# First experts' layer: the copy of the next block's weights moved from ScalarE to VectorE

## The chip, the cores and the metric

One core of one Trainium2 chip. The metric is the device time of one launch of the whole program, in microseconds (us). A core has TensorE (PE; its weight loads are listed apart as PEld), VectorE (DVE), ScalarE (ACT), GpSimd (POOL) and SyncE (SP), which here only issues DMAs. SBUF is the memory on the chip with 128 partitions, PSUM the memory into which TensorE writes.

## The reference

Four layers over a graph of 3125 nodes with 256 features, all in float32: graph attention with a feed-forward network, a mixture of experts, a graph network of two steps, and a second mixture of experts. The change concerns the second, after the router:

```python
for e in range(E):                      # 8 experts, each token goes to 2
    h = jax.nn.gelu(tokens @ w1[e] + b1[e], approximate=False)
    y = h @ w2[e] + b2[e]
    out = out + combine[:, e:e + 1] * y
```

Here `w1[e]` and `w2[e]` are 256 x 256 each.

## The kernel before

The whole program runs its stages one after another. The first experts' layer is `experts(k, 0)` (L1692). Before it the router has given each (token, expert) pair a slot, the slots of one expert lie together, and they are padded to blocks of 256 rows. At most NBLK blocks exist, 30 of them run here, in an order that the chip has computed into the table `ORDER`: a word of it holds the block's slot number and its expert, and `block_of` (L1683) loads the word into registers of an engine (the load itself has line L430).

One block j is worked like this, with every tile double (index b):

- SyncE loads the 256 rows (`load_rows`, L1764), stores the output of block j-2 (`store`, L1775) and loads the bias row for the output (`load_rest`, L1769), in this order within its `step`. Its waits make the load of the next rows stand behind the store of an earlier output in the queue.
- TensorE turns the rows (`turn`, L1940) into `p_turned`; VectorE copies them from PSUM into `turned` (`copy_turned`, L1857).
- TensorE multiplies with the first weights (L1955) into `p_hidden`, in two halves; ScalarE applies the Gelu to each half (L1923) into `hidden`.
- TensorE turns the rows of block j+1, then multiplies `hidden` with the second weights (L1964) into `p_y`; VectorE adds the bias row to it (L1867) in two halves.

So TensorE's order is: first layer of j, turn of j+1, second layer of j, first layer of j+1, and so on.

The weights of all eight experts are loaded once, before the blocks, into the tile `every` (8 x 1026 columns: 512 for the first weights, 512 for the second, 2 for the first bias). The block's own expert must lie at a fixed place for TensorE, so before block j+1 its 1026 columns are copied from `every` to `pack[1 - b]`. Before the change ScalarE does that copy (`copy_weights`, L1912) at the head of its `step` for block j: it waits for `y_done` to reach j, that is until block j-1, the last user of that pack, is through its second layer, copies, signals `copied`, and only then applies the two Gelus of block j. TensorE waits for `copied` before each first layer. ScalarE copies the weights of block 0 ahead of the loop.

GpSimd meanwhile scatters the normalised rows into slots (L1823, 50 indirect DMAs, many of which are before the blocks start), then adds the residual in one TENSOR_TENSOR over all rows (L1833: 128 partitions x 6400 columns), and then gathers the outputs back (L1843) as they become available. The last gathers and VectorE's weighted sums (L1874, L1880) end the stage. The attention and the second experts' layer (`experts(k, 1)`, which loads its weights by DMA into `pack`) are not touched.

`half`, `over_blocks` and `over_odd` write out blocks 0 to 2 and loop over the others in pairs, on each engine alike.

Of the kernel before, what the change touches and what calls it, by code (L numbers as in the profile page):

```python
# [43 lines left out]
NEXP, TOPK = 8, 2  # L44
# [117 lines left out]
def wait_if(eng, sem, value):  # L162

    if not isinstance(value, int) or value > 0:
        eng.wait_ge(sem, value)
# [24 lines left out]
def at(i, n=1):  # L190
    return bass.ds(i, n)
# [234 lines left out]
def table_values(nc, engine, table, lo, most):  # L426


    why = "the chip computed the table within these bounds"
    values = nc.values_load_multi_w_load_instructions(  # L430
        table[0:1, at(lo, len(most))], engines=[engine], min_val=0, max_val=max(most),
        skip_runtime_bounds_check_because=why)[1]
    return [nc.s_assert_within(v, 0, m, skip_runtime_bounds_check_because=why) for v, m in zip(values, most)]
# [1249 lines left out]
def block_of(nc, engine, k, j):  # L1683


    word, = table_values(nc, engine, k["ORDER"], j, [511])
    why = "the chip computed the table within these bounds"
    return (nc.s_assert_within(word & 63, 0, NB - 1, skip_runtime_bounds_check_because=why),
            nc.s_assert_within(word >> 6, 0, NEXP - 1, skip_runtime_bounds_check_because=why))


def experts(k, layer):  # L1692
# [7 lines left out]
    nc, a, C, X, ST = k["nc"], k["a"], k["C"], k["X"], k["ST"]  # L1700
# [5 lines left out]
    G, B2 = B1 + HC, B1 + HC + 2 * KD  # L1706
# [3 lines left out]
    with ExitStack() as s:  # L1710
        def sb(what, shape, dt=F32):
            return s.enter_context(nc.sbuf_tensor(tag + what, shape, dt))

        def sem(what):
            return s.enter_context(nc.semaphore(tag + what))

        pack = k["PACK"] = [sb(f"pack{b}", [P, SIZE]) for b in range(2)]
        pack_in = k["PACK_IN"] = [sem(f"pack_in{b}") for b in range(2)]
        normed = sb("normed", [P, NT, D]) if layer else k["R"][:, 0:NT, :]
        every = None if layer else sb("every", [P, NEXP, G])  # L1720
        every_in, copied = sem("every_in"), sem("copied")
# [14 lines left out]
        hidden_done, gelu_done, y_done = sem("hidden_done"), sem("gelu_done"), sem("y_done")  # L1736
# [6 lines left out]
        order = Order(k, s, tag, pY[1][0], pY[1][1])  # L1743
# [6 lines left out]
        def over_blocks(eng, step):  # L1750
            n = eng.value_load(k["EPAIRS"][0:1, 0:1], min_val=2, max_val=NBLK // 2)
            over_odd(eng, n, step)
            return n

        @block.sync
        def _(sp):
# [33 lines left out]
            if not layer:  # L1790
                for e in range(NEXP):
                    sp.dma_start(every[:, e, :], a[name][e, :, 0:G]).then_inc(every_in, 16)
            sp.wait_ge(order.ready, 1)
            _, e = block_of(nc, mybir.EngineType.SP, k, 0)
            if layer:
                sp.dma_start(pack[0][:, 0:G], a[name][at(e), :, 0:G].squeeze(0)).then_inc(pack_in[0], 16)
# [49 lines left out]
        @block.vector  # L1846
        def _(dve):
            def copy_turned(j, b):
                dve.wait_ge(turned, j + 1)
                wait_if(dve, hidden_done, HC * (j - 1))  # L1850
                if affine:
                    dve.wait_ge(rest_in[b], 16 * (half[0] + 1))
                    for c in range(KD):
                        ins = dve.tensor_scalar(tT[b][:, c, :], pT[:, c, :], rest[b][:, c:c + 1],  # L1854
                                                rest[b][:, KD + c:KD + c + 1], ALU.mult, ALU.add)
                else:
                    ins = dve.tensor_copy(tT[b][:], pT[:])  # L1857
                ins.then_inc(tT_ready, 1)

            def step(j, b, i, first, last):  # L1860
                half[0] = i + b
                copy_turned(j + 1, 1 - b)
                dve.wait_ge(y_done, j + 1)
                dve.wait_ge(rest_in[b], 16 * (i + 1))
                wait_if(dve, y_out[b], 16 * i if not first else 0)
                for r in range(BR):
                    ins = dve.tensor_tensor(y[b][:, r, :], pY[b][r][:, 0:D], rest[b][:, B2 - G:], ALU.add)  # L1867
                ins.then_inc(y_ready, 1)

            def add_first(n):  # L1870
                dve.wait_ge(back_in[n], 16 * TOPK * (layer + 1))
                if not layer:
                    dve.wait_ge(residual, 1)
                dve.scalar_tensor_tensor(out=sums[n % RING][:], in0=back[:, n, 0, :], scalar=k["W12"][:, n, 0:1],  # L1874
                                         in1=X[:, n, :] if layer else normed[:, n, :], op0=ALU.mult,
                                         op1=ALU.add).then_inc(first_done, 1)

            def add_second(n):
                dve.wait_ge(first_done, n + 1)
                dve.scalar_tensor_tensor(out=X[:, n, :], in0=back[:, n, 1, :], scalar=k["W12"][:, n, 1:2],  # L1880
                                         in1=sums[n % RING][:], op0=ALU.mult, op1=ALU.add).then_inc(x_ready, 1)

            def spread_of(n):
                dve.wait_ge(x_ready, n + 1)
                dve.bn_stats(ST[:, n, :], X[:, n, :])

            def normalised(n):
                dve.tensor_scalar(normed[:, n, :], X[:, n, :], rstd[:, n:n + 1], nmr[:, n:n + 1], ALU.mult,  # L1888
                                  ALU.add).then_inc(normed_ready, 1)

            for n in range(2 * GN):
                normalised(n)
            order.vector(dve)
            for n in range(2 * GN, NT):
                normalised(n)
            dve.tensor_scalar(k["CSLOT"][:], k["SLOT"][:], float(NSLOT), None, ALU.is_lt).then_inc(slots_ready, 1)
            dve.wait_ge(slots_ready, 1)
            dve.tensor_tensor(k["CSLOT"][:], k["CSLOT"][:], k["SLOT"][:], ALU.mult).then_inc(slots_ready, 1)
            half = [0]
            copy_turned(0, 0)  # L1900
            over_blocks(dve, step)
            parts = (add_first, add_second) if layer else (add_first, add_second, spread_of)
            for n in range(NT + len(parts) - 1):
                for late, part in reversed(list(enumerate(parts))):
                    if 0 <= n - late < NT:
                        part(n - late)

        @block.scalar
        def _(act):
            def copy_weights(j, b):  # L1910
                _, e = block_of(nc, mybir.EngineType.Activation, k, j)
                act.copy(pack[b][:, 0:G], every[:, at(e), :].squeeze(1)).then_inc(copied, 1)  # L1912

            def step(j, b, i, first, last):
                if layer:
                    if not first:
                        act.wait_ge(y_done, j - 1)
                else:
                    wait_if(act, y_done, j)
                    copy_weights(j + 1, 1 - b)  # L1920
                for h in range(HC):
                    act.wait_ge(hidden_done, HC * j + h + 1)
                    act.activation(hid[b][:, h, :], pH[h % NH][:, 0:BT], ACT.Gelu,  # L1923
                                   bias=pack[b][:, B1 + h:B1 + h + 1]).then_inc(gelu_done, 1)

            act.activation(warm[:], k["EPSC"][:], ACT.Gelu)
            if not layer:
                act.wait_ge(order.ready, 1)
                act.wait_ge(every_in, 16 * NEXP)
                copy_weights(0, 0)  # L1930
            over_blocks(act, step)

        @block.tensor
# [488 lines left out]
```

## Time and profile before

| | |
|---|---|
| median of 3 runs | 2809.07 us (2808.21 to 2824.49) |
| the profiled execution, by the same clock as the runs | 2811.28 us |
| its span, from the first to the last instruction | 2809.5 us |
| granted TensorE clock over the span | 0.923 of full |
| busy: PE, DVE, ACT, POOL | 2291.3, 1475.0, 1228.3, 720.7 us |
| ScalarE's weight copies | 30, 1047 to 1052 ns each, 1399.9 to 1549.2 us |
| Blocks of the layer, first first-layer matmul to last bias add | 1413.4 to 1553.9 us |

All times of instructions are of that one execution and count from the start of its span. "Idle before", in brackets at the end of a timeline row, is the time that the engine stood before the instruction, with an arrow to what released it. A row with xN joins N instructions of one line. A granted clock of 1.00 is 2.4 GHz, 0.50 is 1.2 GHz.

### The profile page before, as it was taken

How to read it: one execution, taken by the hardware profiler on the slowest of the kernel's cores; microseconds unless marked ns; L12 is line 12 of the kernel's file. 1: busy time of each engine (PE TensorE's matmuls, PEld its weight loads, DVE VectorE, ACT ScalarE, POOL GpSimd, SP SyncE). 2: the span in 40 equal slices, each digit the busy share in tenths (PEclk: the TensorE clock that was granted, in tenths of full speed). 3: DMA queues.
4: the chain of work that ended last, by engine and by line, in shares of the span. 5: the costliest groups of instructions: out<-in, count | busy, mean ns of one | idle time of the engine just before them, and what ended most of it. 6: DMA issues, size and time to landing. Idle time of an engine off the chain costs nothing. (4 is left out here: it accounts for less than half of the span.)

```text
span 2809.5 us, 49979 instructions
## 1 busy us (share of the span) xinstructions
PE 2291.3 (82%) x10903; PEld 1803.6 (64%) x10904; DVE 1475.0 (53%) x2939; ACT 1228.3 (44%) x2503; POOL 720.7 (26%) x720
## 2 busy tenths in 40 slices
PE   2788876888888885997378399994999944999995
PEld 1344443666666663886367288883888843888885
DVE  7799975889898986334623644434001064111113
ACT  1799933777777771223233132223222241222221
POOL 0000012777777760002273311000110005102013
PEclk9899997999999998998589699996999956999998
DMA  5412222777777760000266322211222104656555
GB/s 199 195 74 76 76 83 89 208 213 212 213 212 213 212 183 36 1 0 4 85 200 185 107 67 69 71 55 54 71 67 73 49 2 173 218 192 220 191 206 178
DMA packets 183896, 353.27 MB, mean 126 GB/s; under 512 B 55347, under 2 KB 138728, under 8 KB 179112
## 3 DMA queue, kind: packets, MB, share of 16 engines
q1 hardware_dynamic: 138328, 206.94, 22.6%
q0 software_dynamic: 45520, 145.80, 18.2%
q8 instruction: 18, 0.29, 0.0%
q14 instruction: 30, 0.24, 0.0%
HBM read 275.32 MB, written 77.31 MB: 126 GB/s over the span
## 5 line engine op out<-in xcount | busy, mean ns | idle before, releaser
L2200 PE MATMUL gnn_p<-gnn_y,gnn_counts_wide 128*128 (+1 forms) x2500 | 553.0, 381 | 2.7 <-DVE R_kept L2135 2.5
L2200 PEld LDWEIGHTS gnn_p<-gnn_y,gnn_counts_wide 128*128 128x128 f32 x2500 | 472.5, 191 | 69.1 <-DVE R_kept L2135 6.8
L856 POOL DMA_INDIRECT kv_pair<-kv,gather_idx x448 | 427.9, 955 | 150.4 <-issue 101.2
L2071 ACT CAST gnn_counts_wide<-gnn_counts 128x1664 f32<-128x1664 uint16 x100 | 157.9, 1579 | 421.4 <-PE gnn_p L2200 403.7
L956 PE MATMUL p_edge_q<-QX_kept,onehot_turned 128*128 x904 | 264.2, 415 | 62.1 <-ACT onehot_turned L919 55.7
L1923 ACT ACTIVATE experts_hidden<-experts_p_hidden,experts_pack 128x256 f32<-128x256 f32 x290 | 134.3, 473 | 341.5 <-PE experts_p_hidden L1955 341.5
L1955 PE MATMUL experts_p_hidden<-experts_turned,experts_pack 128*128 128x256 f32 x1160 | 264.1, 383 | 2.1 <-DVE experts_turned L1854 1.2
L956 PEld LDWEIGHTS p_edge_q<-QX_kept,onehot_turned 128*128 128x128 f32 x904 | 155.2, 191 | 167.1 <-issue 151.6
L1964 PE MATMUL experts_p_y<-experts_pack,experts_hidden 128*128 128x256 f32 x1160 | 260.9, 380 | 0.0
L1955 PEld LDWEIGHTS experts_p_hidden<-experts_turned,experts_pack 128*128 128x128 f32 x1160 | 223.0, 192 | 33.7 <-issue 2.8
L564 PE MATMUL adj_p<-adj_onehot_src,adj_onehot_key 128*128 128x416 f16 x1200 | 234.4, 346 | 6.8 <-DVE adj_onehot_src L538 4.6
L964 PE MATMUL p_sums<-R_kept 128*128 128x264 f32 x896 | 236.7, 387 | 0.0
L1964 PEld LDWEIGHTS experts_p_y<-experts_pack,experts_hidden 128*128 128x128 f32 x1160 | 216.6, 191 | 27.2
L1843 POOL DMA_INDIRECT experts_back<-slots_out,CSLOT x100 | 97.6, 976 | 418.7 <-issue 417.3
L908 ACT ACTIVATE dst_distance<-WHERE_kept,DST_kept 128x128 f32 x456 | 158.3, 394 | 67.1 <-issue 67.0
L538 DVE TENSOR_SCALAR adj_onehot_src<-adj_count_src,adj_src_in_quarter 128x832 f16<-128x832 f16 x500 | 181.4, 430 | 0.0
L1854 DVE TENSOR_SCALAR experts_turned<-experts_p_turned,experts_rest 128x256 f32<-128x256 f32 x60 | 29.9, 540 | 276.5 <-DMA experts_rest<-experts 249.7
L564 PEld LDWEIGHTS adj_p<-adj_onehot_src,adj_onehot_key 128*128 128x128 f16 x1200 | 110.8, 99 | 96.2 <-issue 6.1
L883 DVE TENSOR_TENSOR qk_prod<-kv_pair,p_edge_q 128x528 f32<-128x528 f32 x224 | 156.5, 698 | 21.1 <-DMA kv_pair<-kv,gather_idx 13.9
L964 PEld LDWEIGHTS p_sums<-R_kept 128*128 128x128 f32 x896 | 153.2, 191 | 14.9 <-DVE ACC_kept L875 0.3
L2174 POOL TENSOR_TENSOR R_kept<-gnn_y,gnn_brows 128x256 f32 x50 | 39.3, 785 | 461.1 <-DVE gnn_y L2111 459.0
L888 DVE TENSOR_REDUCE qk_sum<-qk_prod 128x16 f32<-128x528 f32 x224 | 155.9, 696 | 0.0
(358 smaller groups left out, 3183.3 us busy)
## 6 DMA issues: line engine op xcount, KB each, us to landing
experts_pack<-experts SPq DMA_DIRECT2D x29, 2052.0 KB, 8.7
gnn_counts<-adj SPq DMA_DIRECT2D x400, 104.0 KB, 2.2
adj<-adj_counts SPq DMA_DIRECT2D x100, 208.0 KB, 1.9
experts_rows<-slots_in SPq DMA_DIRECT2D x60, 256.0 KB, 3.6
slots_out<-experts_y SPq DMA_DIRECT2D x58, 256.0 KB, 7.7
experts_rest<-experts SPq DMA_DIRECT2D x60, 130.0 KB, 7.4
kv_pair<-kv,gather_idx POOLq DMA_INDIRECT x448, 3.8
slots_in<-R_kept SPq DMA_DIRECT2D x2, 3328.0 KB, 14.0
```

The source lines that it names most:

```text
L538: ins = dve.tensor_scalar(ohs[p][:, c, :], count[:], column(smod, t + c), None, ALU.is_equal)
L564: mm = pe.matmul(pA[p][:, c, 0:QS // 2], ohk[p][:, n, :], ohs[p][:, n, c * (QS // 2):(c + 1) * (QS // 2)], start=False, stop=False)
L856: pool.indirect_dma_start(kv[r][:, j, :], None, a["kv"], bass.IndirectOffsetOnAxis(ap=idx[r][:, j:j + 1], axis=0)).then_inc(kv_in[r], 16)
L883: dve.tensor_tensor(prod[:], kv[r][:, :, 0:QW], pQ[q][:, :, 0:QW], ALU.mult).then_inc(prod_ready, 1)
L888: dve.tensor_reduce(red[q][:].rearrange("p j h -> p (j h)"), prod[:].rearrange("p j (h c) -> p (j h) c", c=HD + 1), AX.X, ALU.add).then_in ...
L908: ins = act.activation(dist[q][:, j, :], where[:, at(w), :].squeeze(1), ACT.Square, scale=-1.0, bias=column(k["DST"], t + j))
L956: mm = pe.matmul(pQ[q][:, j, 0:QW], oht[q][:, j, :], QX[:, at(w), :].squeeze(1), start=True, stop=True)
L964: mm = pe.matmul(pA[q][:, 0:VW], oh[r][:, j, :], wv[r % 4][:, j, :], start=(j == 0), stop=(j == GT - 1))
L1955: mm = pe.matmul(pH[c][:, 0:BT], w[:, lo:lo + P], tT[b][:, d, :], start=(d == 0), stop=(d == KD - 1))
L1964: mm = pe.matmul(pY[b][r][:, 0:D], hid[b][:, h, r * P:(r + 1) * P], w[:, W2 + h * D:W2 + (h + 1) * D], start=(h == 0), stop=(h == HC - 1))
L2071: act.copy(wide[b][:], raw[r][:].rearrange("p q s -> p (q s)")).then_inc(wide_ready, 1)
L2200: mm = pe.matmul(bank[:, off:off + D], wide[b][:, j * P:(j + 1) * P], y[:, at(n), :].squeeze(1), start=first and off == 0, stop=last and ( ...
```

## The change

VectorE gets `copy_weights`. In its `step` for block j it first copies the turned rows of block j+1, then the weights of block j+1, then adds the bias for block j. It waits for `y_done` to reach j before the copy, as ScalarE did. ScalarE's `step` holds only the two Gelus and waits for `copied` of its own block, because the bias in `pack` is an operand. The copy for block 0 goes to VectorE too, ahead of the first turned rows.

```diff
@@ VectorE @@
+            def copy_weights(j, b):
+                _, e = block_of(nc, mybir.EngineType.DVE, k, j)
+                wait_if(dve, y_done, j - 1)
+                dve.tensor_copy(pack[b][:, 0:G], every[:, at(e), :].squeeze(1)).then_inc(copied, 1)
+
             def step(j, b, i, first, last):
                 half[0] = i + b
                 copy_turned(j + 1, 1 - b)
+                if not layer:
+                    copy_weights(j + 1, 1 - b)
                 dve.wait_ge(y_done, j + 1)
                 dve.wait_ge(rest_in[b], 16 * (i + 1))
...
             half = [0]
+            if not layer:
+                dve.wait_ge(every_in, 16 * NEXP)
+                copy_weights(0, 0)
             copy_turned(0, 0)
             over_blocks(dve, step)
@@ ScalarE @@
-            def copy_weights(j, b):
-                _, e = block_of(nc, mybir.EngineType.Activation, k, j)
-                act.copy(pack[b][:, 0:G], every[:, at(e), :].squeeze(1)).then_inc(copied, 1)
-
             def step(j, b, i, first, last):
                 if layer:
                     if not first:
                         act.wait_ge(y_done, j - 1)
                 else:
-                    wait_if(act, y_done, j)
-                    copy_weights(j + 1, 1 - b)
+                    act.wait_ge(copied, j + 1)
...
             act.activation(warm[:], k["EPSC"][:], ACT.Gelu)
-            if not layer:
-                act.wait_ge(order.ready, 1)
-                act.wait_ge(every_in, 16 * NEXP)
-                copy_weights(0, 0)
             over_blocks(act, step)
```

## Rows read from the trace of the kernel before

**Rows 1.** The page, part 1: engine, busy us, share of the span, instructions.

```profile
PE 2291.3 (82%) x10903; PEld 1803.6 (64%) x10904; DVE 1475.0 (53%) x2939; ACT 1228.3 (44%) x2503; POOL 720.7 (26%) x720
```

**Rows 2.** Line L1857 alone, window 1451 to 1552: shortest, median and longest ns.

```profile
L1857 DVE COPY experts_turned<-experts_p_turned x22: 691/692/693, 1451.5 to 1551.3; 128x512 f32<-128x512 f32 x22
```

**Rows 3.** Timeline behind the loop, GpSimd's first gather there.

```profile
1557.43 0.95 POOL L1843 DMA_INDIRECT experts_back<-slots_out,CSLOT  x1 [27.72 <-issue]
```

**Rows 4.** Timeline of one block, 1455 to 1462: start us, length us, engine, line.

```profile
1455.33 0.66 PE L1940 MATMUL experts_p_turned<-C_kept,experts_rows 128*128 128x128 f32 x4 [0.54 <-DMA experts_rows<-slots_in]
...
1456.11 0.69 DVE L1857 COPY experts_turned<-experts_p_turned 128x512 f32<-128x512 f32 x1 [2.07 <-PE experts_p_turned L1940]
...
1457.33 1.70 PEld L1955 LDWEIGHTS experts_p_hidden<-experts_turned,experts_pack 128*128 128x128 f32 x8
1457.55 1.89 PE L1955 MATMUL experts_p_hidden<-experts_turned,experts_pack 128*128 128x256 f32 x8
1457.91 0.76 DVE L1867 TENSOR_TENSOR experts_y<-experts_p_y,experts_rest 128x256 f32<-128x256 f32 x2 [1.11 <-PE experts_p_y L1964]
1458.26 1.05 ACT L1912 COPY experts_pack<-experts_every 128x1026 f32 x1 [2.86 <-PE experts_p_y L1964]
1458.96 0.40 SPq L1775 DMA_DIRECT2D slots_out<-experts_y  x1
1459.21 0.83 ACT L1923 ACTIVATE experts_hidden<-experts_p_hidden,experts_pack 128x256 f32<-128x256 f32 x2
...
1459.91 0.66 PE L1940 MATMUL experts_p_turned<-C_kept,experts_rows 128*128 128x128 f32 x4 [0.47 <-DMA experts_rows<-slots_in]
1460.29 1.60 PEld L1964 LDWEIGHTS experts_p_y<-experts_pack,experts_hidden 128*128 128x128 f32 x8
...
1461.67 0.38 SPq L1764 DMA_DIRECT2D experts_rows<-slots_in  x1
```

**Rows 5.** The waits, window 1451 to 1553: us in total, times, longest.

```profile
PE experts_p_turned L1940 <- DMA experts_rows<-slots_in: 13.9, 21, 1.4
```

**Rows 6.** Groups by line of VectorE: busy us, mean ns; idle before.

```profile
L2111 DVE COPY gnn_y<-gnn_p 128x256 f32 x44 | 18.7, 425 | 191.2 <-PE gnn_p L2189 191.2
...
L2107 DVE COPY gnn_z<-R_kept 128x256 f32 x22 | 6.2, 283 | 0.0
```

**Rows 7.** Line L430 alone: VectorE's sequencer loading a table entry.

```profile
L430 DVEq TENSOR_LOAD <-GROUPS_kept x225: 299/305/346, 458.7 to 1049.3; - x113
```

**Rows 8.** Timeline, the stage's first turn and first layer.

```profile
1411.43 1.12 PE L1940 MATMUL experts_p_turned<-C_kept,experts_rows 128*128 128x128 f32 x4 [20.23 <-DMA experts_rows<-slots_in]
...
1413.42 3.75 PE L1955 MATMUL experts_p_hidden<-experts_turned,experts_pack 128*128 128x256 f32 x8 [0.88 <-DVE experts_turned L1857]
```

**Rows 9.** Timeline of GpSimd in the loop, around 1451.

```profile
1451.64 13.76 POOL L1833 TENSOR_TENSOR R_kept<-R_kept,X_kept 128x6400 f32<-128x6400 f32 x1 [1.81 <-DMA slots_in<-R_kept,SLOT]
```

**Rows 10.** Line L612 alone, window 368 to 382.

```profile
L612 DVE TENSOR_SCALAR h_row<-X_kept,RSTD_kept,NMR_kept x3: 395/5228/5324, 369.6 to 375.8; 128x256 f32<-128x256 f32 x3
```

**Rows 11.** The timeline there, both engines.

```profile
375.09 5.76 POOL L721 TENSOR_TENSOR WHERE_kept<-C_kept 128x3328 f32<-128x3328 f32 x1 [0.31 <-issue]
375.78 5.23 DVE L612 TENSOR_SCALAR h_row<-X_kept,RSTD_kept,NMR_kept 128x256 f32<-128x256 f32 x1 [0.53 <-PE p_hT L759]
```

**Rows 12.** Timeline of GpSimd, 1391 to 1400.

```profile
1394.26 4.91 POOL L1823 DMA_INDIRECT slots_in<-R_kept,SLOT  x1 [0.30 <-issue]
```

**Rows 13.** Line L1888 alone (VectorE): shortest, median and longest ns.

```profile
L1888 DVE TENSOR_SCALAR R_kept<-X_kept,RSTD_kept,NMR_kept x25: 393/396/412, 1381.8 to 1398.6; 128x256 f32<-128x256 f32 x25
```

**Rows 14.** Stretches: us, busy of PE, PEld, DVE, ACT, POOL, granted clock, DMA.

```profile
1553.00:1556.00 3.00, 0.00 (x0) 0.00 (x0) 2.81 (x8) 0.00 (x0) 0.00 (x0) 1.00 0.25 87
...
1557.00:1558.00 1.00, 0.00 (x0) 0.00 (x0) 1.00 (x4) 0.00 (x0) 0.56 (x1) 0.50 0.03 8
...
1419.00:1420.00 1.00, 1.00 (x5) 0.77 (x5) 0.00 (x0) 0.00 (x0) 0.69 (x2) 0.70 0.08 29
```

**Rows 15.** Groups by line in the stage, window 1411 to 1554.

```profile
L1823 POOL DMA_INDIRECT slots_in<-R_kept,SLOT x31 | 29.8, 962 | 9.4 <-issue 9.1 <-DMA slots_in<-R_kept,SLOT 0.3
```

## The prediction, made before the changed kernel was run

> **What bounds the kernel now.** The page first: 2809.5 us, one stage after another, with TensorE busy 82% of them [rows 1]. The change touches one stage, the 30 blocks of the first experts' layer. VectorE turns 22 of them over between 1451.47 and 1551.35 us, so one takes 99.9/21 = 4.76 us [rows 2], and with the 8 earlier ones the loop runs from 1413 to 1553 us: 140 us, 5% of the span. Nothing else runs beside it that could end the stage: the gathers behind the last blocks start only once the last output has landed [rows 3]. So a microsecond of the loop is a microsecond of the kernel.
>
> Then one block in the timeline [rows 4]. TensorE turns the next block's rows (1455.33), multiplies the second layer of this one (weight loads from 0.38 us after the turn, 1.60 us long), goes straight into the first layer of the next (1457.33, 1.70 us) and then stands until 1459.91, because the next rows have not landed. The waits say the same of the whole stretch: 13.9 us in 21 waits for `experts_rows` [rows 5], and none of TensorE for an activation in this stretch. Followed back, rows arrive late by a loop through the queue: output added (1457.91 to 1458.67), store issued (1458.96), then the rest of a pack and the table entries, next rows issued 2.71 us after the store (1461.67), landed, turned.
>
> ScalarE's copy of 1026 columns is 1.05 us and pushes the two activations back to 1459.21 to 1460.04. The second layer's first weights, which want the first activation (about 1459.7), load at 1460.29, behind the turn. The copy is therefore already hidden, with 0.6 us to spare for the first activation [rows 4].
>
> **The change part by part.**
> *ScalarE loses the copy and the wait for `y_done`.* 29 times 1.05 us of work go, and in the loop nobody waits for it; activations some 0.6 us earlier still find the second layer behind the turn. I take 0. A gain is bounded by the wait for rows: if all 13.9 us were in truth waits for activations, the whole of it scaled to 29 blocks would be 19 us; the row names the rows and I keep none of it.
>
> *VectorE gets the copy, 1026 columns, SBUF to SBUF.* This trace has the same operation with 256 columns in 283 ns, while from PSUM 256 columns are 425 ns and 512 are 692 ns [rows 2, 6]. From PSUM a column is 267/256 = 1.04 ns above a base of 158 ns. At half that per column the SBUF copy would be 158 + 133 = 291 ns, at the full rate 425: so it runs at twice the rate per column. 1026 columns are 158 + 535 = about 0.69 us; at the slow rate 1.23 us.
>
> *Where it lies.* It is queued behind the turned rows (0.69 us, starting 0.78 us after the turn). The table entry that it needs is loaded by the sequencer in 0.3 us [rows 7], beside the copy of the turned rows; not hidden it would be 0.3 us more. Instructions on VectorE overlap by some 0.07 us, so the copy ends 0.78 + 0.62 + 0.69 = 2.09 us after the turn's start. TensorE wants it at 2.00 us (1457.33 less 1455.33) [rows 4]: the first layer slips 0.1 to 0.2 us. TensorE stands 0.66 us a block for rows right after, so that is nearly all absorbed. Ends: 0 and 29 times 0.15 = 4.4 us; I take 0.5. The bias add behind it is due at 2.58 us after the turn, so it doesn't move, and neither does the store loop. The initial copy falls into the idle time before the first rows are turned (1411.43) [rows 8]: 0. Two waits are new. VectorE waits for `y_done` of the block before, which its own bias add has already waited for, so nothing queues behind it; ScalarE waits for `copied` of its own block, which TensorE needs before it can give ScalarE anything: 0 for both.
>
> *The new neighbour.* GpSimd runs one TENSOR_TENSOR over 6400 columns from 1451.64 to 1465.40, 13.76 us, in the middle of the loop [rows 9]. Elsewhere this trace shows what a VectorE instruction of the fast kind meets there. A TENSOR_SCALAR from SBUF to SBUF that takes 395 ns alone takes over 5.2 us twice; the one issued at 375.78 under a GpSimd TENSOR_TENSOR ends at 381.01, 0.16 us after GpSimd's instruction (380.85) [rows 10, 11]. The other way round, a GpSimd DMA_INDIRECT of 0.96 us took 4.91 us beneath VectorE's run of such TENSOR_SCALARs, while these stayed at 393 to 412 ns [rows 12, 13]. The two engines exclude each other for whole instructions. Today VectorE's two instructions in the loop read PSUM and don't care. No row shows a COPY stuck; the 283 ns put it among the fast kind.
>
> The Trainium skill, "SBUF — State Buffer", section Who interferes with whom, names it: copy, cast and tensor_scalar in a two-port mode take the port pair shared with GpSimd, and the one that issues second blocks until the first is done. The trace agrees for TENSOR_SCALAR (5.23 us instead of 0.40); that copies belong to it no row shows. By the rule the time is the forecast's, without it rival A's.
>
> *Its price.* The first weight copy that comes due u us after GpSimd's start ends 0.45 us after GpSimd: the stuck TENSOR_SCALAR ended 0.16 us after it, so 0.24 of its 0.40 us had been spent under the block, and I take as much off the 0.69 us. Unhindered it would end at u + 0.69. So it is 13.76 + 0.45 - 0.69 - u = 13.5 - u late. TensorE waits for it with the first layer, the bias add, store and next rows are queued behind it on VectorE. u is between 0 and one block, 4.76. In this trace the copy would come due at 1452.1, u = 0.45; but GpSimd's scatters before it are themselves held up by the new copies, by 0 to 8 times 0.69 = 5.4 us over eight blocks, which moves u freely. I take the middle, u = 2.4: 11.1 us, ends 8.7 and 13.5. Later copies of the loop are not under it.
>
> *TensorE's clock.* In the stall TensorE stands 9 to 13 us. Behind the loop TensorE has no work from 1553 on; the granted clock is 1.00 until 1556 and 0.50 in 1557 to 1558. At the stage's start, where it works from 1411.43, the clock is 0.70 in 1419 to 1420, on the rise [rows 8, 14]. So in the stall it falls to 1.2 GHz. At that level the first block's first layer took 3.75 us, and its turn 1.12 us, against 1.89 us and 0.66 us [rows 4, 8]. The block after the stall so costs 2 times 1.86 + 0.46 = 4.2 us more; the rows are there by then, which gives 0.66 back: 3.5 us. It could be none (the clock back at once) or the full 4.2 us.
>
> *GpSimd's other work* (scatters and gathers 0.69 us later at most, each time) is followed by no wait of the queue in the loop; 0.
>
> Sum: 11.1 + 3.5 + 0.5 = 15.1 us. On the profiled execution's 2811.3 us that is 2826.4; the median of the runs is 2.2 us below that execution, so 2824.2 us, 0.5% slower.
>
> **The rivals.**
> *A, no collision, not slower than before:* the copy finds GpSimd's long instruction no obstacle, the loop hides 0.69 us as it does now. For: no COPY stands stuck in a row of this trace. Against: the TENSOR_SCALARs of [rows 10, 11]. It decides at 1451.64 us: a weight copy under GpSimd of 0.7 us. Time 2809.07 + 0.5 = 2809.6.
> *B, slow rate, no collision:* the copy takes 1.23 us, ends 2.63 us after the turn, 0.65 to 0.75 us late for TensorE, whose 0.66 us of wait per block swallow most: 0 to 0.2 us a block over 29, some 3 us, 2812 us. Against: 283 ns [rows 6].
> *C, small collisions too:* the copies also wait for GpSimd's DMA_INDIRECTs, of which 31 scatters of 0.96 us alone lie in the stage [rows 15], and as many gathers follow. On perhaps 14 blocks half an instruction, 0.5 us, of which half is absorbed, and some of it also delays the bias add: 3 to 7 us more, about 2829 us. Against: 412 ns as the longest of 25 beside such instructions [rows 12, 13].
> *D, faster:* ScalarE, not the rows, holds the second layer back, and its 0.6 us a block come free: 17 us in 29 blocks, and no collision: 2792 us. For: nothing but the nearness of 1460.04 and 1460.29. Against: [rows 5].
>
> **How the numbers follow.** Forecast 0.78, A 0.07, B 0.05, C 0.08, D 0.02. The forecast's own range is 8.7 + 0 + 0 to 13.5 + 4.2 + 4.4 us, in practice 2818 to 2829. To hold 8 in 10 with the rivals it goes from 2814 (leaving A, B and D, 0.14, out) to 2831. One percent, 28 us, is about what a measurement of this kernel can tell from no change; only C with everything at its upper end, or a collision at a second place, passes it: 0.04. Faster by 1%: 0.01. Within: 0.95.
>
> **What would show it.** Right: one weight copy of VectorE between 9 and 14 us long that ends some 0.2 us after GpSimd's TENSOR_TENSOR, the others 0.69 us; TensorE idle over 8 us before a first layer in that stretch, and the granted clock at 0.50 for the block behind it; blocks elsewhere still 4.7 to 4.8 us apart and still ended by rows; a few scatters of GpSimd longer than 0.96 us. Wrong: all 30 copies near 0.69 us (A), near 1.23 us (B), copies of 1 to 2 us under scatters (C), or a loop pitch under 4.5 us (D). The clock term is wrong if first layers after the stall take 1.89 us.

## The result and the profile after

The changed kernel takes 2821.99 us (median of 7; 2820.45 to 2838.73) against 2808.83 us (median of 7; 2807.22 to 2824.49): ratio 1.006, 95% interval 1.0035 to 1.0085. That is 13 us slower; the forecast was 2824.2 us. A few executions of either kernel are some 16 us longer than the rest (one of the 7 before, two of the 7 after). The profiled execution took 2820.45 us with a span of 2818.7 us, 9.2 us more than the profiled execution before.

First the two copies in the loop, each line alone (count, shortest/median/longest ns, first and last start), profile after:

```profile
L1857 DVE COPY experts_turned<-experts_p_turned x30: 690/692/693, 1410.3 to 1558.8; 128x512 f32<-128x512 f32 x30
...
L1863 DVE COPY experts_pack<-experts_every x30: 689/698/10558, 1401.5 to 1559.5; 128x1026 f32 x30
```

29 of the 30 weight copies are near 0.70 us and one is 10.56 us. The loop, from the first turned rows to the end of the last bias add, is 151.0 us where it was 141.3 us. The timeline shows where the long copy lies:

```profile
1450.53 13.67 POOL L1833 TENSOR_TENSOR R_kept<-R_kept,X_kept 128x6400 f32<-128x6400 f32 x1 [2.10 <-DMA slots_in<-R_kept,SLOT]
...
1452.69 0.66 PE L1941 MATMUL experts_p_turned<-C_kept,experts_rows 128*128 128x128 f32 x4 [0.62 <-DMA experts_rows<-slots_in]
...
1453.48 0.69 DVE L1857 COPY experts_turned<-experts_p_turned 128x512 f32<-128x512 f32 x1 [2.50 <-PE experts_p_turned L1941]
...
1454.19 10.56 DVE L1863 COPY experts_pack<-experts_every 128x1026 f32 x1
1464.67 0.74 DVE L1874 TENSOR_TENSOR experts_y<-experts_p_y,experts_rest 128x256 f32<-128x256 f32 x2
...
1464.88 3.78 PE L1956 MATMUL experts_p_hidden<-experts_turned,experts_pack 128*128 128x256 f32 x8 [9.81 <-DVE experts_pack L1863]
...
1468.45 1.00 PE L1941 MATMUL experts_p_turned<-C_kept,experts_rows 128*128 128x128 f32 x4
...
1469.29 1.89 PE L1965 MATMUL experts_p_y<-experts_pack,experts_hidden 128*128 128x256 f32 x8
...
1470.23 0.74 DVE L1863 COPY experts_pack<-experts_every 128x1026 f32 x1
```

GpSimd's addition, the same as in [rows 9], ends at 1464.20. The copy, issued at 1454.19, ends at 1464.75, 0.55 us after it. The turned rows' copy at 1453.48 runs under the same GpSimd instruction and is not touched: it reads PSUM and takes its usual 0.69 us. Behind the long copy stand the bias add, the store and, through `copied`, TensorE, 9.81 us by its row. Then read how long TensorE's work takes: 3.78 us for the first layer and 1.00 us for the turn, but 1.89 us again for the second layer. The stretches say the same (granted clock third from the end):

```profile
1458.00:1459.00 1.00, 0.00 (x0) 0.00 (x0) 1.00 (x1) 0.00 (x0) 1.00 (x1) 1.00 0.00 0
1459.00:1464.00 5.00, 0.00 (x0) 0.00 (x0) 5.00 (x1) 0.00 (x0) 5.00 (x1) 0.50 0.00 0
...
1468.00:1469.00 1.00, 1.00 (x5) 0.78 (x4) 0.00 (x0) 0.30 (x1) 0.05 (x1) 0.50 0.14 44
1469.00:1471.00 2.00, 2.00 (x11) 1.62 (x9) 1.38 (x2) 0.17 (x1) 1.70 (x2) 0.93 0.61 152
```

The clock falls to 1.2 GHz in the stall. In 1469 to 1471 us it is 0.93 of full speed on average, so it came back at about 1469.3, 4.4 us after TensorE resumed. The waits from 1451 us on, against [rows 5]:

```profile
PEld experts_p_turned L1941 <- DMA experts_rows<-slots_in: 15.8, 19, 2.0
PE experts_p_hidden L1956 <- DVE experts_pack L1863: 9.8, 1, 9.8
PE experts_p_turned L1941 <- DMA experts_rows<-slots_in: 8.5, 13, 1.6
```

Rows still end the other blocks. The turned rows' copies span 148.5 us from the first start to the last, and the long block takes 16.1 us of them (1453.48 to 1469.59); the others are (148.5 - 16.1)/28 = 4.73 us apart, 4.79 before. ScalarE's freedom bought nothing that can be seen. Summed by stage, the 9.2 us between the two profiles are +9.7 in this loop, +1.6 in the first step of the GNN behind it (from the issue of its affine rows to the same issue in the second step), +1.5 in the untouched stages together, and -3.6 us between the start of the router and the first turned rows. That last stretch took 49.5 us in the profile before, 45.9 after, and 45.5 to 46.2 in six of the seven runs below that went to chips of the same speed. The profile before holds the scatter of 4.91 us of [rows 12] there, which stood under VectorE's TENSOR_SCALARs; the seventh run (e10, early rows with the whole addition) has one of 4.90 us and takes 49.9 us too. So the change did not earn these 3.6 us, and the 13.2 us between the medians are the better measure of it.

### The profile page after: what moved, and what is told of

Read it like the earlier page. It is cut to its first block and busy times, and to the rows that moved or that the text cites. A ratio compares the mean times of both kernels' runs of the same rounds, so it can differ in the third digit from the quotient of the medians.

```text
span 2818.7 us, 49981 instructions
## 1 busy us (share of the span) xinstructions
PE 2294.4 (81%) x10903; PEld 1800.4 (64%) x10904; DVE 1506.5 (53%) x2969; ACT 1202.6 (43%) x2473; POOL 718.0 (25%) x720
## 5 line engine op out<-in xcount | busy, mean ns | idle before, releaser
L1956 PE MATMUL experts_p_hidden<-experts_turned,experts_pack 128*128 128x256 f32 x1160 | 268.0, 387 | 13.2 <-DVE experts_pack L1863 10.8
```

The source lines that it names most:

```text
L1956: mm = pe.matmul(pH[c][:, 0:BT], w[:, lo:lo + P], tT[b][:, d, :], start=(d == 0), stop=(d == KD - 1))
```

## The experiments

My theory: VectorE's SBUF-to-SBUF copy and a GpSimd instruction exclude each other, and the stall with its clock is the loss. The rival: the place in VectorE's queue costs in every block. Times are compared with the kernel before on the same chip. The intervals below reach 4 to 7 us to either side, so differences of a few us are read from the stages of the profiles, of which each kernel has one.

**Leaving GpSimd's addition out.** In both kernels:

```diff
-                pool.tensor_tensor(normed[:], normed[:], X[:, 0:NT, :], ALU.add).then_inc(residual, 1)
+                pool.sem_inc(residual, 1)
```

> The changed kernel without GpSimd's residual addition (6400 columns; the output of the first experts' layer so lacks its residual), a mere signal in its place. Lock theory (VectorE's SBUF-to-SBUF copy and a GpSimd instruction exclude each other): the one copy of 10.56 us goes back to 0.70 us, all 30 lie between 0.69 and 0.90 us, the time falls from 2822 to 2808 to 2811 us. Rival (the place in VectorE's queue costs: the first layer slips about 0.5 us in every block, and the stall is only part of the loss): at least 3 us stay, 2812 to 2815 us.

> The kernel before, with the same piece of work left out. Both theories: no instruction of the loop waits for GpSimd there, so 2808 to 2810 us as before; it is the partner of the run above, and their difference is the price of moving the copy without any collision: under 1.5 us by the lock theory, 3 us or more by the rival.

Line L1863 alone in the changed kernel without the addition:

```profile
L1863 DVE COPY experts_pack<-experts_every x30: 686/698/922, 1400.9 to 1549.5; 128x1026 f32 x30
```

The long copy is gone, and the loop is 141.0 us with the moved copy and 140.7 us without it: 0.2 us for 29 blocks. The whole times, however, missed both expectations: 2819.84 us (ratio 1.0046, 1.0031 to 1.0062) and 2816.63 us (1.0031, 1.0015 to 1.0048) against 2807.44 us. In both runs the stretch from the second experts' layer's last turned rows to the end is about 46 us instead of 36, presumably because the missing residual changes what that layer routes. So the pair must be read against each other, and there 3.2 us stay, as the rival had it, though not in the loop. The profiles put them elsewhere, below.

**The copy at the single rate.** A form with one SBUF source that isn't of the fast kind:

```diff
-                dve.tensor_copy(pack[b][:, 0:G], every[:, at(e), :].squeeze(1)).then_inc(copied, 1)
+                dve.tensor_reduce(pack[b][:, 0:G], every[:, at(e), :].squeeze(1).unsqueeze(2), AX.X,
+                                  ALU.max).then_inc(copied, 1)
```

> The changed kernel with the copy written as a TENSOR_REDUCE (max over one element), a form that should run at the single rate: some 1.23 us instead of 0.70 for each of the 30, in the same place of the queue, with GpSimd's residual addition in place. Lock theory: the lock belongs to the fast kind alone, so none of the 30 is longer than 1.3 us, there is no stall, and the time is 2810 to 2817 us although VectorE works longer. Rival (whatever VectorE reads from SBUF under GpSimd's instruction is held up, or the queue is what costs): one copy over 9 us again, or 0.5 us more in every block, 2822 us or more.

The line alone, then GpSimd's and VectorE's timeline in that run:

```profile
L1863 DVE TENSOR_REDUCE experts_pack<-experts_every x30: 1222/1222/1224, 1399.6 to 1548.9; 128x1026 f32 x30
```

```profile
1447.65 13.74 POOL L1833 TENSOR_TENSOR R_kept<-R_kept,X_kept 128x6400 f32<-128x6400 f32 x1 [2.11 <-DMA slots_in<-R_kept,SLOT]
```

```profile
1452.62 1.22 DVE L1863 TENSOR_REDUCE experts_pack<-experts_every 128x1026 f32 x1
```

1.22 us under the full length of GpSimd's instruction, as everywhere else. VectorE works 0.52 us longer in every block and the kernel is faster: 2811.8 us, ratio 1.0025 (1.0005 to 1.0045), loop 142.4 us. Same place in the queue, same source and destination, same neighbour: what costs is the kind of the instruction, the fast COPY. The run changes rate and operation together, so it does not show which of the two matters. The rival falls for the loop.

**GpSimd's addition in 25 instructions.**

```diff
-                pool.tensor_tensor(normed[:], normed[:], X[:, 0:NT, :], ALU.add).then_inc(residual, 1)
+                for n in range(NT):
+                    ins = pool.tensor_tensor(normed[:, n, :], normed[:, n, :], X[:, n, :], ALU.add)
+                ins.then_inc(residual, 1)
```

> The changed kernel with GpSimd's residual addition in 25 instructions of 256 columns, one per tile of rows. Lock theory, the lock held for one instruction: a copy waits for the piece under way, 0.8 us at most, so the longest copy is under 2 us and the time 2808 to 2812 us. Rival (GpSimd keeps the pair over its back-to-back instructions, or it is the amount of its work that counts): a copy of about 10 us stays and with it 2822 us.

```profile
L1865 DVE COPY experts_pack<-experts_every x30: 686/698/1025, 1399.6 to 1547.8; 128x1026 f32 x30
```

The longest copy is 1.03 us, the loop 140.7 us, the time 2809.9 us, ratio 1.0019 (1.0002 to 1.0036). The lock (the exclusion of one engine by the other) is held for one instruction, and VectorE gets in between two of them; a piece of GpSimd that meets a copy takes up to 1.18 us instead of 0.72.

**The addition twice in a row** (the residual so counts double; the second waits for the first one's semaphore; one execution alone):

> The changed kernel with GpSimd's residual addition done twice in a row (the residual so counts double, the output of the layer is changed by that). Lock theory: the copy that comes due under the first addition waits for it, about 10 us as before; the second addition follows a semaphore later, so either the same copy also waits for it (one copy of 22 to 25 us) or the copy gets in between and the next one is stuck for 8 to 13 us (two long copies). Either way the stage is 9 to 14 us longer than the changed kernel's 151.0 us from first turned rows to last output. Rival (a single hiccup at the point where the scatters end, whatever GpSimd does next): 151 us again.

This run, the two with 19 and 22 idle instructions and the two with 48 memsets (e5, e6, e7, e11, e12) went to chips on which the kernel before takes 3158 to 3181 us; the attention takes 882 to 904 us there instead of 635, and the first blocks of our loop wait for scattered rows. Their whole times and loops can't be set beside the others; single instructions can. GpSimd's timeline, then VectorE's:

```profile
1707.59 13.66 POOL L1833 TENSOR_TENSOR R_kept<-R_kept,X_kept 128x6400 f32<-128x6400 f32 x1 [1.61 <-DMA slots_in<-R_kept,SLOT]
1721.33 14.01 POOL L1835 TENSOR_TENSOR R_kept<-R_kept,X_kept 128x6400 f32<-128x6400 f32 x1
```

```profile
1713.36 8.45 DVE L1865 COPY experts_pack<-experts_every 128x1026 f32 x1
1721.72 0.74 DVE L1876 TENSOR_TENSOR experts_y<-experts_p_y,experts_rest 128x256 f32<-128x256 f32 x2
...
1727.14 8.76 DVE L1865 COPY experts_pack<-experts_every 128x1026 f32 x1
```

Two additions, two stuck copies. The first ends 0.56 us after the first addition (1721.81 against 1721.25) and had its turn before the second: that one started at 1721.33, while the copy was running, and took 14.01 us instead of 13.66. The exclusion works both ways, and this is the expectation's second branch (8 to 13 us each). That the loop grows by 9 to 14 us could not be read on this chip.

**Where the other 2 to 3 us are.** With the pieces nothing is stuck and the loop is no longer than before, and yet the kernel is 2.5 us slower. Stage by stage all variants with the copy on VectorE have the excess in one place, the first step of the GNN, which no edit touches: 349.5 to 350.6 us, against 347.9 us in both kernels with the copy on ScalarE. There the matmuls wait for the affine rows (`brows`): TensorE stands 1.6 us for them after the change, and its weight loads 2.0 us instead of 0.2. The DMAs of its first 5 us, before and then after (queues: packets, MB, share; issues: count, KB, us to landing):

```profile
q1 hardware_dynamic: 532, 0.99, 64.3%
...
gnn_brows<-rows_g SPq DMA_DIRECT2D x1, 384.0 KB, 3.3
```

```profile
q14 instruction: 1, 0.01, 0.6%
...
gnn_brows<-rows_g SPq DMA_DIRECT2D x1, 384.0 KB, 5.1
```

One packet of an instruction queue, by its name a piece of program being fetched, lies in that window after the change and not before, and the transfer lands 1.8 us later. Is it the program's length that moved it there, and which engine's? The kernel before with padding on VectorE, and the pieces with padding on ScalarE, each ahead of the first block:

```diff
+                for c_ in range(19):
+                    dve.memset(sums[0][:, c_:c_ + 1], 0.0)
```

```diff
-            act.activation(warm[:], k["EPSC"][:], ACT.Gelu)
+            for c_ in range(1 if layer else 22):
+                act.activation(warm[:, c_:c_ + 1], k["EPSC"][:], ACT.Gelu)
```

> The kernel before with 19 one-column memsets more on VectorE in its idle time ahead of the first block (some 2 us, hidden), as many instructions as the change adds to VectorE's program. Code theory (the 1.5 to 2.7 us that the first GNN layer takes longer in every variant with the moved copy come from where an instruction fetch falls: 2 us behind that stage's start, beside the transfer of its three affine rows, which then lands in 5.1 us instead of 3.3; and it is VectorE's program that has been shifted): the layer's first step is 350 us instead of 347.9, that transfer 5.1 us, the time 2810 us. If it is ScalarE's program: 347.9 us, 3.3 us and 2808 us.

> The changed kernel with the residual in 25 pieces and 21 one-column activations more on ScalarE ahead of the first block, as many instructions as the change takes from ScalarE's program. Code theory with ScalarE's program as the shifted one: the fetch goes back, the transfer of the affine rows lands in 3.3 us again, the GNN layer's first step is 348 us and the time 2807 to 2808 us. With VectorE's as the shifted one: 350 us, 5.1 us and 2810 us as without the padding.

The first of these, in the 4 us around the step's start in its own profile:

```profile
q14 instruction: 1, 0.01, 0.5%
...
gnn_brows<-rows_g SPq DMA_DIRECT2D x1, 384.0 KB, 5.2
```

With the copy still on ScalarE, 19 idle instructions on VectorE bring the packet and the 5.2 us, and the step takes 350.1 us. Padding ScalarE changes nothing: the packet is there, 5.3 us and 350.3 us. So it goes with VectorE's program, as far as one padding of each engine can show. Ratios: 1.0018 (1.0001 to 1.0036) and 1.0017 (1.0000 to 1.0035). The reverse, 48 memsets on VectorE in the kernel with the pieces:

> The changed kernel with the residual in 25 pieces (no stall) and 48 one-column memsets more on VectorE ahead of the first block, in its idle time. Code theory (the instruction fetch beside the start of the first GNN layer belongs to VectorE's program and costs that layer 1.5 to 2.7 us by where it falls): 48 instructions further on the fetch falls into the loop or the sums before, the transfer of the affine rows lands in 3.3 us, the layer's first step is 348 us instead of 350.4, and the time is that of the kernel before within 1 us. Rival (the excess comes with anything that moves the copy to VectorE): 350 us and 2 to 3 us above the kernel before.

```profile
q1 hardware_dynamic: 327, 0.71, 55.6%
...
gnn_brows<-rows_g SPq DMA_DIRECT2D x1, 384.0 KB, 3.5
```

No instruction packet there now, 3.5 us to landing, and the step is 348.9 us, 1.5 us of the 2.5 back (348 was expected). So packet and landing follow VectorE's padding in both directions. The whole time, ratio 1.0003 (0.9986 to 1.0020), decides nothing: its interval overlaps that of the pieces without padding, and the runs of one kernel spread over 18 to 24 us on that chip. How a packet that itself takes 0.3 to 0.5 us goes with a landing 1.8 us later stays open.

**Does a free ScalarE pay once rows are early?** SyncE loads the rows one block ahead, past the wait for `y_done` and the store (and block 0's ahead of the loop):

```diff
-                e = load_rows(j, b, j - 1)
+                load_rows(j + 1, 1 - b, j)
+                _, e = block_of(nc, mybir.EngineType.SP, k, j)
```

> The kernel before (ScalarE copies) with SyncE's load of the rows issued one block earlier, ahead of the wait for y_done and the store of an earlier output, in the first experts' layer alone. If the late rows are what sets the pace of 4.8 us a block (as I read the waits), TensorE's own work does: 1.70 and 1.60 us of weight loads, the turn's 0.4, gaps of 0.25 us, about 3.95 us as between blocks 1 and 2 of the changed kernel's profile; ScalarE's chain (y_done, 0.5 us, copy 1.05 us, first activation 0.47 us) ends just as the turn does, so it costs at most 0.3 us more. 4.0 to 4.3 us a block, 14 to 24 us less: 2785 to 2795 us on a chip where the kernel before takes 2808. Rival (ScalarE's copy sets the pace): 4.7 us a block stays, 2808 us.

> The changed kernel with the residual in 25 pieces (no long lock) and the rows one block earlier. TensorE then waits for VectorE's weight copy, which ends 0.79 + 0.70 + 0.16 + 0.70 = 2.35 us behind the start of the turn, and loads weights 0.1 us later: 2.45 + 1.7 = 4.15 to 4.25 us a block, 0.1 to 0.3 us more than with the copy on ScalarE (3 to 8 us over 29 blocks): 2790 to 2798 us. Rival (the change's idea: with ScalarE free of the copy a loop that no longer waits for rows runs at TensorE's 3.95 us, and the moved copy pays): faster than the run above by 3 us or more.

> The changed kernel as it is, with the rows one block earlier. Lock theory: the gain of the earlier rows and the stall add up, since a copy comes due under GpSimd's addition whatever the pace: one copy of 9 to 13 us, and 10 to 13 us more than the run with the pieces.

The kernel before with early rows: 2796.13 us, ratio 0.9944 (0.9922 to 0.9965), loop 130.2 us instead of 141.3: the rows did set the pace. Both expected ranges were missed by a little: 4.40 us a block instead of 4.0 to 4.3, and 1 us above 2795. With the copy on VectorE and the pieces: 2800.10 us (0.9972, 0.9948 to 0.9997), though its loop is shorter, 128.5 us. That fits neither branch: the loop was expected to be 3 to 8 us longer, and the rival wanted 3 us less in the whole. The waits of the first show what is left over, from 1440 to 1530 us:

```profile
DVE experts_y L1876 <- DMA experts_rest<-experts: 7.5, 5, 1.8
PE experts_p_turned L1949 <- DMA experts_rows<-slots_in: 5.5, 6, 1.5
...
PEld experts_p_y L1973 <- ACT experts_hidden L1932: 0.4, 1, 0.4
```

ScalarE, copy included, held TensorE up by 0.4 us in some 20 blocks; rows still do, by 5.5 us in 6 waits. With the copy on VectorE and the pieces, two edits at once, the loop gains 1.7 us by the profiles, and the GNN's first step loses 1.1 us (349.1 against 348.0, the packet is there again). The 4 us between the medians go against it, but the two intervals overlap, so that difference is not shown.

The third, with the whole addition, has one stuck copy:

```profile
L1872 DVE COPY experts_pack<-experts_every x30: 689/698/13249, 1416.6 to 1569.9; 128x1026 f32 x30
```

It takes 2809.36 us, 9.3 us above the pieces, just under the expected 10 to 13. In its profile the copy starts u = 0.96 us after the addition, almost the worst case. (That execution spent 16 us more in the attention, ahead of all this, and holds the scatter of 4.90 us, so its u need not be that of the others.)

The last run put all of it together.

> The same with the rows loaded one block earlier, as the candidate that takes all that the runs showed: no long lock, no late rows, no fetch at the GNN layer's start. Stage 128.5 us from first turned rows to last output, the GNN layer's first step 348 us; 2793 to 2796 us, 1 to 3 us under the kernel before with the early rows (2796.1). If the fetch theory is wrong: 2800 us as without the padding.

The GNN's step is 348.2 us, as expected; the whole, 3161.34 us, is not to be told from the kernel before (1.0001, 0.9983 to 1.0020), which on that chip says nothing on the loop, whose rows come late from the scatter. Whether it beats 2796.1 us on the other chips wasn't measured. Both versions with early rows and no stuck copy are shown to beat the kernel before; the fastest median is that of the kernel before with the early rows.

## Why the prediction was right, and where its terms were off

- *The stall.* Right in mechanism, and the formula gave the size: u was 1454.19 - 1450.53 = 3.66 us, 13.5 - u = 9.8, and the copy was 10.56 - 0.70 = 9.86 us late. That it fits to 0.1 us is luck: the copy ended 0.55 us after GpSimd, not 0.45 (nor the 0.2 among the prediction's signs), and the addition took 13.67 us, not 13.76. With the measured numbers in place of the two, the formula also fits the 12.55 us of e10 and the 7.75 us of the first stuck copy of e5, to 0.1 us. The term itself, 11.1 us, was 1.3 us too large through u alone. The scatters were held up by 1.1 us in sum before the addition (it starts 41.3 us after the stage's first turn, 40.2 before), not by the 2.7 that the middle stood for (eight times 0.69 is 5.5, not 5.4); from u = 0.45 even that was enough to let one more copy pass ahead of the addition, so that the next one met it.
- *The clock.* 3.5 us were stated. The mechanism was right, but the step "the block after the stall costs 2 times 1.86 + 0.46" failed: after this stall the clock stayed low for 4.4 us, and only the first layer and the turn fell under it. Against 1.99 us (the span of a first layer that starts after a wait, in the blocks beside it) and 0.66 us, that is 1.8 + 0.3 = 2.1 us, less 0.66 for rows already there: 1.4 us. The model for it, the 8 us at the stage's start in the trace before, was one case of many: the same start took 5.5 us in the changed kernel's own profile.
- *The slip.* 0.5 us in sum; 0.2 us by the pair without the addition. Its inside was off: TensorE starts 0.13 us after the copy's end (1464.75 and 1464.88), which the sum left out. In the blocks behind the stall its weight loads start 1.53 us (median) after the turned rows' copy, 1.22 before, so the first layer slipped by 0.3 us, not 0.15. The wait for rows absorbed it as stated.
- *ScalarE's relief, 0.* Right: the loop without stall is as long as before, and with early rows ScalarE, copy included, held TensorE up by 0.4 us.
- *Missing.* The 1.6 us of the GNN's first step (2.5 us with the pieces). No step of mine looked at what a longer program does to the fetch of code. Stall 9.8, clock 1.4 and slip 0.2 make 11.4 us for that one block; the other 28 blocks gave 1.7 us back, which in the kernel without addition they did not, so it is scatter. 11.4 - 1.7 + 1.6 = 11.3 us stand against 13.2 between the medians, within the interval. In part the total of 15.1 us came as near as it did by luck: stall and clock were 3.4 us too high, and the 1.6 us were not in it.
- *Rivals.* A and B fall with the 10.56 us and the 0.70 us (B's copy would have ended 0.63 us late for TensorE by its own numbers, not 0.65 to 0.75). C falls: in the changed kernel the longest copy beside a DMA_INDIRECT is 0.89 us. D falls with the rows' waits, and with the 11 us that early rows gave while the copy was still on ScalarE.

## What to carry to other kernels

Before moving work to VectorE, look at what GpSimd does in the same stretch. Here an SBUF-to-SBUF COPY that came due under the long TENSOR_TENSOR waited for its end, in all four cases, so its price was what was left of the neighbour, not its own length; beside a DMA_INDIRECT it lost 0.2 us at most in the changed kernel. The cures that worked were cutting the neighbour into pieces and a slower form of the copy. Work that is already hidden is worth little to its engine when a transfer ends the block: issuing the rows one block earlier was worth 11 us in the loop, and no run shows the kernel gaining from a freed ScalarE. And where a variant is 2 us slower than its stages explain, compare the untouched stages and the instruction queue's packets.

## What the hardware showed that was not expected

- A single 8 KB instruction packet beside the start of a 384 KB transfer goes with a later landing in all 14 profiles: 4.9 to 5.4 us in the nine that have the packet there, 3.2 to 3.7 us in the five that don't; and 19 idle instructions on VectorE were enough to bring that about.
- The time at 1.2 GHz after TensorE resumes is not a constant. Behind the four stalls it was 4.4, 4.7, 5.2 and 5.5 us. At the stage's start, with the same work each time, it was 4.8 to 8.2 us in the nine profiles on chips of the same speed. What decides it no run here shows, so one such start is a poor model for a stall.
- The copy's last 0.55 us run after GpSimd's end (0.55 or 0.56 in all four stuck copies), of 0.70 us in all; the stuck TENSOR_SCALAR of 0.40 us had needed 0.16 us. So 0.15 and 0.24 us were spent under the lock; that this is a fixed part of each instruction is a guess.
